# Ternary weights made in the long convolution's head loop and kept in DRAM until the ternary stage

## The reference, cut to what matters

```python
def weight_quant(w):
    scale = 1.0 / jnp.clip(jnp.mean(jnp.abs(w)), 1e-05)
    return jnp.clip(jnp.round(w * scale), -1.0, 1.0) / scale

def bitlinear158(x, w, b):
    xq = act_quant(rms_norm(x))          # 8-bit rows
    return jnp.einsum('bsd,od->bso', xq, weight_quant(w)) + b
# w1: 2048 x 512, w2: 512 x 2048
```

## Time and profile before

| | us |
|---|---|
| Runs of the kernel (median of 3; lowest, highest) | 2445.17 (2442.45, 2447.16) |
| The profiled execution, and its span | 2443.69, 2441.9 |
| Head loop of the long convolution | 1854 to 2042 |
| Ternary stage, before the first Silu | 2080 to 2138 |
| Ternary stage, from the first Silu on | 2138 to 2442 |

### The profile page before, as it was taken

How to read it: one execution, slowest core, us unless ns; L and a number is a source line. 1 busy time by engine, 2 the same in 40 slices (tenths; PEclk the granted TensorE clock), 3 DMA queues, 4 the chain that set the end, 5 groups by cost and what they waited for, 6 DMA issues and landing times. The chain is left out here.

```text
span 2441.9 us, 34261 instructions
## 1 busy us (share of the span) xinstructions
PE 1885.2 (77%) x12688; PEld 1451.1 (59%) x12688; DVE 1536.7 (63%) x3007; ACT 900.1 (37%) x1525; POOL 476.0 (19%) x478
## 2 busy tenths in 40 slices
PE   3248888614376899999999959999959997178885
PEld 2225555413254799999999948877747775034442
DVE  8747776296475556665666645565635777357876
ACT  1005555500031444444444432222222002567774
POOL 0023232000001000100010001101004766024442
PEclk9859999856587999999999979999978998588897
DMA  5099999212463112222222131100032113601000
GB/s 189 0 147 142 151 150 153 81 48 77 166 207 109 52 54 75 62 68 70 77 66 71 53 107 43 36 18 27 10 107 88 44 44 132 247 0 35 27 22 22
DMA packets 149823, 199.95 MB, mean 82 GB/s; under 512 B 13472, under 2 KB 92192, under 8 KB 147232
## 3 DMA queue, kind: packets, MB, share of 16 engines
q1 hardware_dynamic: 138400, 176.84, 28.8%
q10 hardware_dynamic: 11264, 20.98, 2.3%
HBM read 151.37 MB, written 46.14 MB: 81 GB/s over the span
## 5 line engine op out<-in xcount | busy, mean ns | idle before, releaser
L453 DVE TENSOR_REDUCE a_rowmax<-a_ring 128x2 f32<-128x512 f32 x256 | 165.1, 688 | 99.8 <-PE a_ring L532 97.6
L1463 DVE TENSOR_TENSOR f_hid<-f_gate,f_gu 128x256 f32<-128x256 f32 x264 | 108.5, 420 | 163.6 <-ACT f_gate L1335 161.1
L1335 ACT ACTIVATE f_gate<-f_gu 128x256 f32<-128x256 f32 x264 | 98.7, 383 | 275.3 <-PE f_gu L1201 187.2
L2185 PE MATMUL e_py<-e_kv,e_toep 128*128 128x320 f32 x640 | 180.2, 437 | 0.0
L405 ACT ACTIVATE a_prob<-a_sT 128x1024 f32<-128x1024 f32 x128 | 130.6, 1026 | 80.2 <-PE a_sT L521 80.1
L2185 PEld LDWEIGHTS e_py<-e_kv,e_toep 128*128 128x128 f32 x640 | 119.9, 191 | 46.2 <-issue 0.8
L1214 PE MATMUL f_gu<-f_lowh,f_bg 128*128 128x256 f32 x704 | 141.2, 283 | 5.3 <-POOL f_lowl L1120 5.0
L1201 PE MATMUL f_gu<-f_xhi,f_wg 128*128 128x256 f32 x704 | 130.3, 282 | 0.0
L1201 PE MATMUL f_gu<-f_xhi,f_wu 128*128 128x256 f32 x704 | 129.1, 281 | 0.0
L1214 PEld LDWEIGHTS f_gu<-f_lowh,f_bg 128*128 128x128 f32 x704 | 115.6, 191 | 9.7 <-POOL f_lowl L1120 5.2
L1468 DVE TENSOR_TENSOR f_hl<-f_hid,f_hh 128x768 fp32r<-128x768 f32 (+2 forms) x90 | 84.5, 939 | 55.9 <-ACT f_hh L1381 54.8
(11 more groups left out here) (366 smaller groups left out, 4991.3 us busy)
## 6 DMA issues: line engine op xcount, KB each, us to landing
f_entry<-in_WdT SPq DMA_DIRECT2D x89, 256.0 KB, 2.8
a_qs<-parts SPq DMA_DIRECT2D x96, 128.0 KB, 6.4
a_ks<-parts SPq DMA_DIRECT2D x96, 128.0 KB, 7.0
parts<-a_hi SPq DMA_DIRECT2D x16, 512.0 KB, 8.7
parts<-a_lo SPq DMA_DIRECT2D x16, 512.0 KB, 9.1
e_toep<-in_taps SPq DMA_DIRECT2D x32, 256.0 KB
f_entry<-in_Bg SPq DMA_DIRECT2D x89, 64.0 KB, 1.9
f_entry<-in_Bu SPq DMA_DIRECT2D x89, 64.0 KB, 2.0
```

The source lines that it names most:

```text
L453: dve.tensor_reduce(rowmax[:, s % 2, :, e * SLOTS + j], ring[n % RING][:, :].rearrange("p (q t) -> p q t", t=T), AX.X, ALU.max, negate=Tru ...
L1335: act.activation(gate[:, i % 2, :], gu[n % 3][:, 0, :], ACT.Silu).then_inc(s_["gate_ready"], 1)
L1463: dve.tensor_tensor(hid[:, j, :], gate[:, i % 2, :], gu[n % 3][:, 1, :], ALU.mult).then_inc(s_["hid_ready"], 1)
L2185: last = pe.matmul(py[n % RING][:, 0:DIAG * BS], toep[:, h % 3, (t - j) * P:(t - j + 1) * P], kv[:, h % 2, j, :], start=(j == 0), stop=(j ...
```

## The change

In the long convolution SP loads each weight piece twice, ScalarE takes magnitudes at heads 3 to 10 and scales at heads 15, 17, ..., 29, GpSimd does one all-reduce after the adds of head 12, VectorE makes the means at head 14 and clamps and rounds one piece after each of heads 16, 18, ..., 30, and SP stores each bf16 piece (512 KiB) to a DRAM scratch tensor. The ternary stage loads the eight finished pieces; its own preparation is gone. The mean and inverse are kept in SBUF between the stages. Core of the diff:

```diff
+SCRATCH |= {"ternary": ([2 * KT, P, INNER], BF16)}
@@ long_convolution
+    PIECES = 2 * KT
+    MEAN_AT, SCALE_AT, ROUND_AT = 14, 15, 16
+        wraw = mk.sb("e_wraw", [P, 2, INNER])
+        wq = mk.sb("e_wq", [P, 2, INNER], BF16)
 SP:
+                def load_piece(m):
+                    if 2 <= m < PIECES + 2:
+                        sp.wait_ge(s_["wsum_ready"], m - 1)
+                    elif m >= PIECES + 2:
+                        sp.wait_ge(s_["w_ready"], m - PIECES - 1)
+                    ... (w1 or w2 piece m % 8 into wraw[:, m % 2, :])
+                def send_piece(c):
+                    sp.wait_ge(s_["w_ready"], c + 1)
+                    sp.dma_start(io["ternary"][c], wq[:, c % 2, :]).then_inc(sent_w[c % 2], 16)
                 for h in range(3, SH):
                     sp.wait_ge(s_["y_done"], (h - 2) * KT)
                     taps(h)
+                    if h - 3 < PIECES:
+                        load_piece(h - 3)
+                    c = (h - SCALE_AT) // 2
+                    if (h - SCALE_AT) % 2 == 0 and 0 <= c < PIECES:
+                        load_piece(PIECES + c)
+                    c = (h - ROUND_AT - 3) // 2
+                    if (h - ROUND_AT - 3) % 2 == 0 and 0 <= c < PIECES - 1:
+                        send_piece(c)
+                for c in range(PIECES - 1, PIECES):
+                    send_piece(c)
 GpSimd, after the adds of head h:
+                    if h == MEAN_AT - 2:
+                        pool.wait_ge(s_["wsum_ready"], PIECES)
+                        pool.partition_all_reduce(wall[:, :], wsum[:, :], P, bass.bass_isa.ReduceOp.add).then_inc(s_["wall_ready"], 1)
 ScalarE, after the wraps of head h:
+                    c = h - 3
+                    if 0 <= c < PIECES:
+                        act.activation(wq[:, c % 2, :], wraw[:, c % 2, :], ACT.Abs, accum_out=wsum[:, c:c + 1]
+                                       ).then_inc(s_["wsum_ready"], 1)
+                    c = (h - SCALE_AT) // 2
+                    if (h - SCALE_AT) % 2 == 0 and 0 <= c < PIECES:
+                        act.activation(wraw[:, c % 2, :], wraw[:, c % 2, :], ACT.Identity, scale=winv[:, c // KT:c // KT + 1]
+                                       ).then_inc(s_["w_scaled"], 1)
 VectorE, after the products of head h:
+                    if h == MEAN_AT:
+                        dve.wait_ge(s_["wall_ready"], 1)
+                        ... (means and inverses of w1 and w2)
+                    c = (h - ROUND_AT) // 2
+                    if (h - ROUND_AT) % 2 == 0 and 0 <= c < PIECES:
+                        dve.wait_ge(s_["w_scaled"], c + 1)
+                        ws.step(dve.tensor_scalar(wraw[:, c % 2, :], wraw[:, c % 2, :], -1.0, 1.0, ALU.max, ALU.min))
+                        if c >= 2:
+                            dve.wait_ge(sent_w[c % 2], 16 * (c // 2))
+                        dve.tensor_scalar(wq[:, c % 2, :], wraw[:, c % 2, :], ROUND, -ROUND, ALU.add, ALU.add
+                                          ).then_inc(s_["w_ready"], 1)
@@ ternary_feedforward, SP
-                for k in range(KT):
-                    sp.dma_start(pieces[k], io["w1"][k * P:(k + 1) * P, :]).then_inc(got_w[k], 16)
                 (x tiles 0 and 1, then b1)
                 for k in range(KT):
-                    sp.dma_start(pieces[KT + k]...
+                    sp.dma_start(w1[:, k, :], io["ternary"][k]).then_inc(s_["got_w1"], 16)
                 (gain, shift, b2)
+                for k in range(KT):
+                    sp.dma_start(w2[:, k * 4:(k + 1) * 4, :], io["ternary"][KT + k].rearrange("p (j o) -> p j o", o=D)
+                                 ).then_inc(s_["got_w2"], 16)
                 (x tiles 2 to 7)
 the rest: magnitudes, scaled, ternary, the two all-reduces and silu's wait for w_ready are removed
```

More of the change, by code:

```diff
@@ L2020, in long_convolution @@
     BACK = 6
+    PIECES = 2 * KT
+    MEAN_AT, SCALE_AT, ROUND_AT = 14, 15, 16
+    held = ExitStack()
+    fix = Maker(nc, held)
+    wmean, winv = fix.sb("g_wmean", [P, 2]), fix.sb("g_winv", [P, 2])
+    keep["ternary"] = dict(held=held, wmean=wmean, winv=winv)
     with ExitStack() as ctx:
@@ L2043, in long_convolution @@
         got_t = [sem(f"e_got_t{u}") for u in range(3)]
+        got_w = [sem(f"e_got_w{u}") for u in range(2)]
+        sent_w = [sem(f"e_sent_w{u}") for u in range(2)]
         stored = sem("e_stored")
@@ L2092, in _ @@
                                  io["x4"][m * 4 * P:(m + 1) * 4 * P, :].rearrange("(n p) f -> p n f", p=P)).then_inc(got_r[m], 16)
+                for u in range(2):
+                    sp.wait_ge(sent_w[u], 16 * KT)
             @block.gpsimd
@@ L2232, in _ @@
                                           ).then_inc(s_["z_ready"], 1)
+                    if h == MEAN_AT:
+                        dve.wait_ge(s_["wall_ready"], 1)
+                        for n in range(2):
+                            mean = wmean[:, n:n + 1]
+                            wm.step(dve.tensor_reduce(mean, wall[:, n * KT:(n + 1) * KT], AX.X, ALU.add))
+                            wm.step(dve.tensor_scalar(mean, mean, 1.0 / (D * INNER), 1e-5, ALU.mult, ALU.max))
+                            dve.reciprocal(winv[:, n:n + 1], mean).then_inc(s_["winv_ready"], 1)
+                    c = (h - ROUND_AT) // 2
+                    if (h - ROUND_AT) % 2 == 0 and 0 <= c < PIECES:
+                        dve.wait_ge(s_["w_scaled"], c + 1)
+                        ws.step(dve.tensor_scalar(wraw[:, c % 2, :], wraw[:, c % 2, :], -1.0, 1.0, ALU.max, ALU.min))
+                        if c >= 2:
+                            dve.wait_ge(sent_w[c % 2], 16 * (c // 2))
+                        dve.tensor_scalar(wq[:, c % 2, :], wraw[:, c % 2, :], ROUND, -ROUND, ALU.add, ALU.add
+                                          ).then_inc(s_["w_ready"], 1)
                 def finish(n):
@@ L2268, in ternary_feedforward @@
     XT = 8
-    with ExitStack() as ctx:
+    own = keep["ternary"]
+    wmean, winv = own["wmean"], own["winv"]
+    with own["held"], ExitStack() as ctx:
         mk = Maker(nc, ctx)
@@ L2350, in root @@
                     pool.tensor_tensor(row[:, n + 2:n + 3], row[:, n + 1:n + 2], keep["neghalf"][:, :], ALU.pow).then_inc(done, 1)
[L2352 to L2355, removed]
                 pool.wait_ge(s_["rows_in"], 64)
@@ L2380, in _ @@
             def _(act):
[L2381 to L2391, removed]
                 act.wait_ge(s_["minus_ready"], 1)
-                magnitudes(0)
-                scaled(0)
-                magnitudes(1)
                 def silu(t):
                     act.wait_ge(s_["h_done"], t + 1)
-                    if t < 3:
-                        act.wait_ge(s_["w_ready"], 2 * KT)
-                    else:
+                    if t >= 3:
                         act.wait_ge(s_["gained"], t - 2)
@@ L2461, in _ @@
                         else:
-                            pe.wait_ge(s_["w_ready"], KT)
+                            pe.wait_ge(s_["got_w1"], 16 * KT)
                         for n in range(QB):
@@ L2504, in scales @@
                     ch.step(dve.tensor_scalar(row[:, 7:8], row[:, 5:6], row[:, 2:3], 127.0, ALU.mult, ALU.mult))
[L2506 to L2521, removed]
                 xs, ys, tails = Chain(dve, s_["x_steps"]), Chain(dve, s_["y_steps"]), Chain(dve, s_["tail_steps"])
                 dve.memset(minus[:, :], -ROUND).then_inc(s_["minus_ready"], 1)
-                ternary(0)
+                dve.tensor_scalar(wfac[:, :], winv[:, 0:1], 127.0, None, ALU.mult).then_inc(s_["wfac_ready"], 1)
                 dve.wait_ge(s_["wfac_ready"], 1)
```

34 lines of the change are left out of this document (17 added, 17 removed).

## The result

| kernel | median us (runs) | ratio to before, 95% |
|---|---|---|
| before | 2446.61 (12) | |
| changed | 2443.28 (12) | 0.9977 [0.9967, 0.9988] |

The change gains 0.23%, 5.6 us by the ratio (2.9 to 8.1). The forecast was 2445.4, no change; the interval leaves a ratio of 1 out, so the kernel has become faster, by little. The profiled execution took 2440.97 us (span 2439.2), 2.7 less than the one of before.

The account below looks back on a forecast made before the run. TensorE was taken to bound the head loop, bytes and then GpSimd the ternary stage's start. Terms -28.4 + 18 + 8.6 + 2 = +0.2 us gave 2445.4 us, no change; 8-in-10 range 2429 to 2457.

Parts of the forecast that it names:

- B: Long convolution from head 16: VectorE's clamp and rounding take turns with GpSimd's adds, 2.3 us a pair; +18 us.
- A: Start of ternary stage without its preparation: b2 lands earlier, no all-reduce, first Silu not waiting for VectorE; -28.4 us.
- the 7.1 us of "issue": Start of ternary stage before the change: GpSimd's own delay after its all-reduce, past b2's landing; 7.1 us.
- The 2.1 for the last head: End of the long convolution's loop: the last rounding stands before products already waiting; 2.1 us more.
- C: Long convolution, GpSimd's all-reduce after head 12: 7.3 us into it, 8.96 out; 8.6 us late at head 16's end.
- rival 1: Loop: the port isn't what limits, TensorE bridges the all-reduce's delay except 6.8 us; sum -21.2, 2424 us; chance 0.17.
- D: Long convolution: piece loads on SP delay the taps from head 5 to 10, ScalarE's work is hidden; +2 us.
- rival 2: Loop from head 16: VectorE loses every turn to GpSimd's adds, 33.6 us; sum +15.8, 2461 us; chance 0.15.

Follow-up runs that it names:

- e4: Kernel before, with both all-reduces of its ternary stage replaced by a TensorE matmul with ones; 2434.83 us, ratio 0.9957.
- e1: Changed kernel, with the column sums of the magnitudes by one TensorE matmul with ones instead of GpSimd's all-reduce; 2429.82 us, ratio 0.9934.
- e2: Changed kernel, with clamp and rounding on ScalarE (four passes) instead of VectorE; 2426.74 us, ratio 0.9927.
- e6: Changed kernel, with GpSimd's first add of a head made as two of 128x512; 2436.08 us, ratio 0.9944.
- e10: e3 with SP's load and store of a piece one head later; 2430.94 us, ratio 0.9942 to the kernel before.
- e3: Changed kernel, with clamp ahead of the last tile of even heads and rounding ahead of that of odd ones, on VectorE; 2447.10 us, ratio 0.9998.
- e5: Changed kernel with the edits of e1 and e2 together; 2419.39 us, ratio 0.9887 to the kernel before.
- e11: Changed kernel, with the eight-column all-reduce after head 12 made as two of four columns; 2444.44 us, ratio 0.9991.
- e8: e5 with pieces 2 to 7 loaded by ScalarE, plus ternary-stage waits moved to the data's first use; 2405.48 us, ratio 0.9827 to the kernel before.

## Why the prediction failed

The forecast was no change, and the time fell by 5.6 us. One term of the sum was mis-sized, B, the roundings between the heads. With 9.5 in place of 18 the sum is -8.3 us; the two stages show -9.0 in the traces.

**A, right:** -27.1 against -28.4. b2 landed 1.3 us later than the sum of bytes said (18.7 for 17.4), and TensorE's first bias matmuls took 5.98 us at a mean granted clock of 0.60 (4.85 at 0.73 in the trace before). Against it stands a gain that the prediction didn't count: ScalarE's table load of 1.28 us, ahead of the first Silu before, now runs while TensorE works. e4 shows by itself the 7.1 us of "issue" that were counted.

**B, the step that failed:** 18 us were forecast, 9.5 measured (lateness from head 16 to 30; 10.1 in e1, 0 in e2). The mechanism stands (e2, e6, e10), the size doesn't. The prediction played the turns from a GpSimd that has finished head 15: clamp, first add, rounding, second add, taps. In the traces GpSimd still owes the third add when the clamp starts, and since it works in order, that short add (0.73) and not the first (2.36) comes between clamp and rounding, and the first add meets the taps' instruction. So VectorE waits for one long add a pair and not for a long and a middle one. The prediction named this order and gave it 14.5; it is 13.9, below its range, because it didn't replay the rest of the sequence behind the changed first turn. That is 0.95 us too much in each of 7 pairs, 6.7. The 2.1 for the last head weren't paid either: lateness goes from 19.7 to 19.8 there, as no products for a next head follow. 8.7 together.

**C, right:** 9.0 against 8.6; into the all-reduce 6.42 (taken: 7.3), out 9.48 (8.96). Why it isn't given back was told only half: in e2 VectorE isn't the bound afterwards, and the 9.5 us from head 12 to 16 all stay, since TensorE has no gap to make up with. That corrects rival 1, which let TensorE bridge all but 6.8. That the sum came out so close is in part luck: 7.3 was the middle of 0 to 14.6, taken for want of a row. The figure of the GPSIMD Engine Reference in the Trainium skill (section Instruction dispatch, about 6 us for the first call of freshly loaded code) is near the way in, 6.42, though no run shows that code is loaded there; the way out took 9.5, and by 5.95 both ways C would have been 4.8 too small.

**D, right within wide bounds:** 1.2 for 2. Lateness reaches 4.5 at head 10, and VectorE makes it up to 1.2 by head 12. Seven kernels with the same work on these engines up to head 12 (the changed one, e1 to e3, e5, e10, e11) show 0.1 to 3.9.

**The rest of the difference:** VectorE's last product of head 0 comes 39.1 us after the stage's start, 2.7 earlier than before (41.9). In kernels equal up to there it varies from 38.6 to 42.7 us, and e4, whose code up to there is that of before, has 38.6: scatter that no step could hold. Behind the loop 1.1 us more are lost until the ternary stage, where the prediction had 0.

**The rivals:** rival 1 (the port isn't what limits, pairs of 12.55) is refuted by pairs of 13.9 and by e6, where cutting GpSimd's add alone shortens them; rival 2 (every turn lost, 17 us a pair) by the rows of one pair.

## What to carry to other kernels

Work put into another engine's idle time costs by the instruction it delays, not by its length: play the turns over two rounds from the state the loop settles in, and after each changed turn replay what follows; then choose the place so that the waiting instruction is a short one (e10), or cut the long one (e6). Count an all-reduce on GpSimd as 16 us between ordinary instructions (16.3 and 17.2 here), and let a matmul with ones do it where TensorE is at hand. And before moving work out of a stage, look at the stage's first wait: GpSimd waited for rows it needs three steps later, and moving such waits to the first use brought 11.3 us in e8, twice what the whole change did. That was measured with the preparation already gone; in the kernel before it wasn't tried.

## What the runs showed of the hardware

- GpSimd's way back from an all-reduce to ordinary instructions is longer than the way in: 9.48 and 9.50 against 6.42 and 6.85 us, all under "issue", with no instruction in the profile.
- A 2048-wide rounding to bf16 on VectorE takes 1.23 us alone and took 1.73 waiting included (e10), and the taps' instruction of 0.34 us anything up to 2.43, by when it asked: the spread of a short instruction's duration is the sign of turns.
- TensorE's first eight bias matmuls, behind a pause of 32.85 us and four small matmuls, took 5.98 us at a mean granted clock of 0.60, that is, for most of that time at the lower of the two levels, 1.2 GHz (in e8, behind a pause of 21.21 us, 6.18 at 0.58). In both kernels the next eight took 3.67 us at 1.00, 2.4 GHz.
